# Splitting nearly every DMA transfer of a linear-attention and mixture-of-experts layer into smaller ones

## What is computed

```python
x = x + attn(layernorm(x), Wqkv, bqkv, Wout, bout, slopes)
x = x + ffn(layernorm(x), w_gate, wi_0, wi_1, wo)

# attn: q, k, v = split(x @ Wqkv + bqkv), per head, in blocks of the sequence
scores = einsum('bhid,bhjd->bhij', qb, kb) * intra_decay
o      = einsum('bhij,bhjd->bhid', scores, vb) + einsum('bhid,bhde->bhie', qb * q_decay, S)
S      = blk_decay * S + einsum('bhjd,bhje->bhde', kb * k_decay, vb)
# then out @ Wout + bout

# ffn: logits = x @ w_gate; the top 2 of 8 experts, weights = softmax(top 2 logits)
out = sum over the 2 experts of weight * ((silu(x @ wi_0[e]) * (x @ wi_1[e])) @ wo[e])
```

## Time and profile before

| | us |
|---|---|
| median of 3 runs | 6599.29 |
| lowest and highest run | 6589.15 and 6755.89 |
| the profiled execution | 6538.36 |
| its span on the slowest core (core 7) | 6536.4 |
| PE busy in the span | 3099.4 (47%) |
| DVE busy | 889.0 (14%) |
| ACT busy | 889.4 (14%) |
| DMA traffic | 732.70 MB, mean 112 GB/s |

### The profile page before, as it was taken

How to read it: one execution, slowest core, us unless ns; L and a number is a source line. 1 busy time by engine, 2 the same in 40 slices (tenths; PEclk the granted TensorE clock), 3 DMA queues, 4 the chain that set the end, 5 groups by cost and what they waited for, 6 DMA issues and landing times.

```text
span 6536.4 us, 39888 instructions; the slowest of 8 cores (6456.9 to 6536.4 us)
## 1 busy us (share of the span) xinstructions
PE 3099.4 (47%) x13620; PEld 1341.5 (21%) x13620; DVE 889.0 (14%) x1577; ACT 889.4 (14%) x2498; POOL 0.2 (0%) x4
## 2 busy tenths in 40 slices
PE   0002063063052142142637761444448888888887
PEld 0001021021021021021213320111113333333333
DVE  1111101101101101111010002221111111111111
ACT  1001012021021021030140011442110000000000
POOL 0000000000000000000000000000000000000000
PEclk9999575575575575565758885556769998999999
DMA  6664624514525425425211113002332111112111
GB/s 189 240 218 163 210 87 147 199 71 167 186 82 174 162 90 189 165 97 177 87 65 52 52 61 132 1 1 94 119 145 93 65 67 50 52 65 78 58 58 77
DMA packets 181569, 732.70 MB, mean 112 GB/s; under 512 B 13144, under 2 KB 13401, under 8 KB 142460
## 3 DMA queue, kind: packets, MB, share of 16 engines
q10 hardware_dynamic: 73728, 369.13, 16.4%
q1 hardware_dynamic: 107648, 361.03, 15.8%
HBM read 579.10 MB, written 151.01 MB: 112 GB/s over the span
## 4 chain that ended last, share of the span: by engine, by line
PE 42%; DMA 29%; ACT 10%; DVE 10%; issue 7%; ACTq 1%; SPq 0%; DVEq 0%
DMA s_cvf<-wffn_im 19%; PE pb L409 4%; PE pb L411 4%; PE pb L947 4%; DMA s_wqcf<-wqkv 4%; PE pb L949 4%; DVE s_cvb L298 4%; PE pb L903 3%; PE pb L904 3%; PE pb L905 3%; PE pb L906 3%; DMA s_wcg<-wqkvb 3%; PE pb L521 3%; PE pb L523 3%; PE pb L340 2%
## 5 line engine op out<-in xcount | busy, mean ns | idle before, releaser
L409 PE MATMUL pb<-s_wcg,s_lnT 128*128 128x512 bf16 x1536 | 610.4, 397 | 1315.8 <-ACT s_kvst L428 1143.2
L411 PE MATMUL pb<-s_wcg,s_lnT 128*128 128x512 bf16 x1536 | 608.5, 396 | 0.0
L340 PE MATMUL pb<-s_ident,s_lntile 128*128 128x128 bf16 x512 | 135.7, 265 | 984.6 <-ACT s_lntile L330 742.6
L947 PE MATMUL pb<-s_wo,s_inter 128*128 128x512 bf16 x1024 | 402.8, 393 | 237.8 <-DVE s_out L962 208.6
L409 PEld LDWEIGHTS pb<-s_wcg,s_lnT 128*128 128x128 bf16 x1536 | 156.2, 102 | 1521.8 <-issue 1357.1
L298 DVE CAST s_cvb<-s_cvf 128x2048 bf16<-128x2048 f32 x192 | 235.6, 1227 | 1419.0 <-DMA s_cvf<-wffn_im 1419.0
L903 PE MATMUL pb<-s_lnT,s_wi 128*128 128x512 bf16 x1024 | 394.7, 385 | 26.3 <-DMA s_wi<-wall 14.3
L949 PE MATMUL pb<-s_wo,s_inter 128*128 128x512 bf16 x1024 | 402.8, 393 | 0.0
L904 PE MATMUL pb<-s_lnT,s_wi 128*128 128x512 bf16 x1024 | 394.7, 385 | 0.0
L905 PE MATMUL pb<-s_lnT,s_wi 128*128 128x512 bf16 x1024 | 394.7, 385 | 0.0
L906 PE MATMUL pb<-s_lnT,s_wi 128*128 128x512 bf16 x1024 | 394.4, 385 | 0.0
(11 more groups left out here) (124 smaller groups left out, 2862.1 us busy)
## 6 DMA issues: line engine op xcount, KB each, us to landing
s_cvf<-wffn_im ACTq DMA_DIRECT2D x192, 1024.0 KB, 6.0
s_wcg<-wqkvb SPq DMA_DIRECT2D x60, 2048.0 KB, 12.3
wall<-s_cvb ACTq DMA_DIRECT2D x192, 512.0 KB, 2.9
s_wi<-wall ACTq DMA_DIRECT2D x128, 512.0 KB, 4.3
s_wqcf<-wqkv SPq DMA_DIRECT2D x16, 3072.0 KB, 15.4
s_wostr<-woutb SPq DMA_DIRECT2D x64, 512.0 KB, 3.4
s_wo<-wall SPq DMA_DIRECT2D x16, 2048.0 KB, 9.2
wqkvb<-s_wqcb SPq DMA_DIRECT2D x16, 1536.0 KB, 6.7
```

Of the source, the lines that this page charges most:

```text
L340: t.inc(ten.transpose(pbankb(bk, P), s_lntile[:, par * C + ch * P: par * C + (ch + 1) * P], s_ident[:]), pe)
L409: ten.matmul(pbank(2 * pt4, 512), lhs, s_wcg[:, i * KB:i * KB + 512], start=st_, stop=False)
L411: ten.matmul(pbank(2 * pt4 + 1, 512), lhs, s_wcg[:, i * KB + 512:(i + 1) * KB], start=st_, stop=False)
L947: ten.matmul(pbank(ybanks[0], 512), lhs, wosl[:, hc * KB: hc * KB + 512], start=st_, stop=sp)
```

## The change

Nearly every large transfer is issued as several smaller ones, each with its own completion increment on the same semaphore. Who issues, what is waited for, the buffers and the arithmetic stay. Transfers that move a row of a matrix per partition are cut by columns, so each piece still has 128 rows but shorter ones; the loads of `s_wcg` and `s_wo` are cut by blocks of rows, and their rows stay 2 KB.

| transfer | before | now | row before, now |
|---|---|---|---|
| load Wqkv | 3 MB | 6 x 0.5 MB | 24 KB, 4 KB |
| store wqkvb | 1.5 MB | 3 x 0.5 MB | 12 KB, 4 KB |
| load expert weights | 1 MB | 2 x 0.5 MB | 8 KB, 4 KB |
| store wall | 0.5 MB | 2 x 0.25 MB | 4 KB, 2 KB |
| load token tile (all three places) | 1 MB | 4 x 0.25 MB | 8 KB, 2 KB |
| load `s_wcg` half | 2 MB | 4 x 0.5 MB | 2 KB, 2 KB |
| load Wout, store woutb | 1 MB, 0.5 MB | 2 pieces each | halved |
| load `s_wostr` | 0.5 MB | 2 x 0.25 MB | 4 KB, 2 KB |
| store x1, load x1, store y | 1 MB | 2 x 0.5 MB | 8 KB, 4 KB |
| load `s_wi` (two per block) | 0.5 MB | 2 x 0.25 MB each | 4 KB, 2 KB |
| load `s_wo` | 2 MB | 4 x 0.5 MB | 2 KB, 2 KB |

The core of the diff (the other places are cut in the same way):

```diff
+    def dma2(eng, out_ap, in_ap, sem, cols, nsplit):
+        step = cols // nsplit
+        for k in range(nsplit):
+            t.inc(eng.dma_start(out=out_ap[:, k * step:(k + 1) * step],
+                                in_=in_ap[:, k * step:(k + 1) * step]), sem, 16)
+        return t.count[sem]
...
-        t.inc(sync.dma_start(out=s_wqcf[:, par * 3 * C:(par + 1) * 3 * C],
-                             in_=d_wqkv[i * P:(i + 1) * P, :]), dQp[par], 16)
+        dma2(sync, s_wqcf[:, par * 3 * C:(par + 1) * 3 * C],
+             d_wqkv[i * P:(i + 1) * P, :], dQp[par], 3 * C, 6)
...
-            t.inc(scal.dma_start(out=s_cvf[:, par * C:(par + 1) * C],
-                                 in_=d_wffn[i * P:(i + 1) * P, :]), dEp[par], 16)
+            dma2(scal, s_cvf[:, par * C:(par + 1) * C], d_wffn[i * P:(i + 1) * P, :],
+                 dEp[par], C, 2)
...
-            t.inc(scal.dma_start(out=d_wall[i * P:(i + 1) * P, :],
-                                 in_=s_cvb[:, par * C:(par + 1) * C]), dDp[par], 16)
+            for k in range(2):
+                t.inc(scal.dma_start(out=d_wall[i * P:(i + 1) * P, k * KB:(k + 1) * KB],
+                                     in_=s_cvb[:, par * C + k * KB: par * C + (k + 1) * KB]),
+                      dDp[par], 16)
...
-                src = d_wqkvb[hf * KB:(hf + 1) * KB, colbase:colbase + KB].rearrange(
-                    "(c p) n -> p c n", p=P)
-                dst = s_wcg[:, hf * 8 * KB:(hf + 1) * 8 * KB].rearrange("p (c n) -> p c n", n=KB)
-                t.inc(sync.dma_start(out=dst, in_=src), dWp[hf], 16)
+                for kk in range(4):
+                    src = d_wqkvb[hf * KB + kk * 2 * P: hf * KB + (kk + 1) * 2 * P,
+                                  colbase:colbase + KB].rearrange("(c p) n -> p c n", p=P)
+                    dst = s_wcg[:, (hf * 8 + 2 * kk) * KB:(hf * 8 + 2 * kk + 2) * KB].rearrange(
+                        "p (c n) -> p c n", n=KB)
+                    t.inc(sync.dma_start(out=dst, in_=src), dWp[hf], 16)
...
-        t.inc(scal.dma_start(out=s_wi[:, par * C:(par + 1) * C], in_=d_wall[r0:r0 + P, :]), dFp[par], 16)
+        dma2(scal, s_wi[:, par * C:(par + 1) * C], d_wall[r0:r0 + P, :], dFp[par], C, 2)
```

More of the change, by code:

```diff
@@ L274, in build_program @@
         t.wait(sync, dv, wq_cvt[i])
-        t.inc(sync.dma_start(out=d_wqkvb[i * P:(i + 1) * P, :],
-                             in_=s_wqcb[:, par * 3 * C:(par + 1) * 3 * C]), dQs[par], 16)
+        for k in range(3):
+            t.inc(sync.dma_start(out=d_wqkvb[i * P:(i + 1) * P, k * 2 * KB:(k + 1) * 2 * KB],
+                                 in_=s_wqcb[:, par * 3 * C + k * 2 * KB: par * 3 * C + (k + 1) * 2 * KB]),
+                  dQs[par], 16)
         wq_st[i] = t.count[dQs[par]]
@@ L367, in build_program @@
                 t.wait(sync, dv, ln_state["stats_dv"].get(pt - 2, 0))
-            t.inc(sync.dma_start(out=s_xstr[:, par * C:(par + 1) * C],
-                                 in_=d_xp[pt * P:(pt + 1) * P, :]), dXp[par], 16)
+            dma2(sync, s_xstr[:, par * C:(par + 1) * C], d_xp[pt * P:(pt + 1) * P, :],
+                 dXp[par], C, 4)
             x_ev[pt] = t.count[dXp[par]]
@@ L475, in build_program @@
             t.wait(sync, dv, own_stats[tt - 2])
-        t.inc(sync.dma_start(out=s_xstr[:, par * C:(par + 1) * C],
-                             in_=d_x[tt * P:(tt + 1) * P, :]), dXp[par], 16)
+        dma2(sync, s_xstr[:, par * C:(par + 1) * C], d_x[tt * P:(tt + 1) * P, :],
+             dXp[par], C, 4)
         xev = t.count[dXp[par]]
@@ L499, in build_program @@
             t.wait(sync, pe, wcg_user[0])
[L500 to L503, removed]
+            for kk in range(4):
+                src = d_wqkvb[hf * KB + kk * 2 * P: hf * KB + (kk + 1) * 2 * P,
+                              cg * KB:(cg + 1) * KB].rearrange("(c p) n -> p c n", p=P)
+                dst = s_wcg[:, (hf * 8 + 2 * kk) * KB:(hf * 8 + 2 * kk + 2) * KB].rearrange(
+                    "p (c n) -> p c n", n=KB)
+                t.inc(sync.dma_start(out=dst, in_=src), dWp[hf], 16)
             wcg_ld[hf] = t.count[dWp[hf]]
@@ L562, in build_program @@
             t.wait(sync, pe, qkv_mm_done[(5, 1)])
-        t.inc(sync.dma_start(out=s_cvf2[:, par * C:(par + 1) * C],
-                             in_=d_wout[i * P:(i + 1) * P, :]), dQp[par], 16)
+        dma2(sync, s_cvf2[:, par * C:(par + 1) * C], d_wout[i * P:(i + 1) * P, :],
+             dQp[par], C, 2)
         t.wait(vec, dQp[par], t.count[dQp[par]])
@@ L571, in build_program @@
         t.wait(sync, dv, wo_cvt[i])
-        t.inc(sync.dma_start(out=d_woutb[i * P:(i + 1) * P, :],
-                             in_=s_cvb2[:, par * C:(par + 1) * C]), dVw[par], 16)
+        for k in range(2):
+            t.inc(sync.dma_start(out=d_woutb[i * P:(i + 1) * P, k * KB:(k + 1) * KB],
+                                 in_=s_cvb2[:, par * C + k * KB: par * C + (k + 1) * KB]),
+                  dVw[par], 16)
         wo_st[i] = t.count[dVw[par]]
@@ L720, in build_program @@
                 t.wait(sync, pe, wostr_used[tpi * NCH + i - 2])
-            t.inc(sync.dma_start(out=s_wostr[:, wpar * C:(wpar + 1) * C],
-                                 in_=d_woutb[i * P:(i + 1) * P, :]), dGp[wpar], 16)
+            dma2(sync, s_wostr[:, wpar * C:(wpar + 1) * C], d_woutb[i * P:(i + 1) * P, :],
+                 dGp[wpar], C, 2)
             lev = t.count[dGp[wpar]]
@@ L764, in build_program @@
             t.wait(sync, dv, resid_ev[tt])
-            t.inc(sync.dma_start(out=d_x1[tt * P:(tt + 1) * P, :],
-                                 in_=s_x1t[:, par * C:(par + 1) * C]), dOp[par], 16)
+            for k in range(2):
+                t.inc(sync.dma_start(out=d_x1[tt * P:(tt + 1) * P, k * KB:(k + 1) * KB],
+                                     in_=s_x1t[:, par * C + k * KB: par * C + (k + 1) * KB]),
+                      dOp[par], 16)
             x1_dma[tt] = t.count[dOp[par]]
@@ L831, in build_program @@
             t.wait(sync, dDp[1], e_ffncv_st[1])
-        t.inc(sync.dma_start(out=s_out[:, tt * C:(tt + 1) * C], in_=d_x1[tt * P:(tt + 1) * P, :]), dS, 16)
+        dma2(sync, s_out[:, tt * C:(tt + 1) * C], d_x1[tt * P:(tt + 1) * P, :], dS, C, 2)
         seed_ev[tt] = t.count[dS]
@@ L854, in emit_wi_load @@
         r0 = e * 3 * M + hc * P
-        t.inc(scal.dma_start(out=s_wi[:, par * C:(par + 1) * C], in_=d_wall[r0:r0 + P, :]), dFp[par], 16)
+        dma2(scal, s_wi[:, par * C:(par + 1) * C], d_wall[r0:r0 + P, :], dFp[par], C, 2)
         r1 = e * 3 * M + M + hc * P
-        t.inc(scal.dma_start(out=s_wi[:, (2 + par) * C:(3 + par) * C], in_=d_wall[r1:r1 + P, :]), dFp[par], 16)
+        dma2(scal, s_wi[:, (2 + par) * C:(3 + par) * C], d_wall[r1:r1 + P, :], dFp[par], C, 2)
         wi_dma[(e, hc)] = (par, t.count[dFp[par]])
@@ L869, in emit_wo_load @@
         r0 = e * 3 * M + 2 * M
-        src = d_wall[r0:r0 + M, cs * KB:(cs + 1) * KB].rearrange("(h p) n -> p h n", p=P)
-        dst = s_wo[:, par * NHC * KB:(par + 1) * NHC * KB].rearrange("p (h n) -> p h n", n=KB)
-        t.inc(sync.dma_start(out=dst, in_=src), dGp[par], 16)
+        for k in range(4):
+            src = d_wall[r0 + k * 2 * P: r0 + (k + 1) * 2 * P,
+                         cs * KB:(cs + 1) * KB].rearrange("(h p) n -> p h n", p=P)
+            dst = s_wo[:, (par * NHC + 2 * k) * KB:(par * NHC + 2 * k + 2) * KB].rearrange(
+                "p (h n) -> p h n", n=KB)
+            t.inc(sync.dma_start(out=dst, in_=src), dGp[par], 16)
         wo_dma[(e, cs)] = (par, t.count[dGp[par]])
@@ L969, in build_program @@
         t.wait(sync, dv, y_evac[(NE - 1, tt, 1)])
-        t.inc(sync.dma_start(out=d_y[tt * P:(tt + 1) * P, :], in_=s_out[:, tt * C:(tt + 1) * C]),
-              dOp[tt % 2], 16)
+        for k in range(2):
+            t.inc(sync.dma_start(out=d_y[tt * P:(tt + 1) * P, k * KB:(k + 1) * KB],
+                                 in_=s_out[:, tt * C + k * KB: tt * C + (k + 1) * KB]),
+                  dOp[tt % 2], 16)
     if DEBUG_TAPS:
```

## The result

The split kernel is slower. Its runs against those of the kernel before, on the same chip, give a ratio of 1.030 with a 95% interval of 1.021 to 1.040; the medians of all runs are 6862.29 and 6666.71 us. On the 6599 us of the kernel before that the forecast used, 1.030 is some 6797 us. The forecast was 6640 us, range 6540 to 6745, and no change with a chance of 0.85.

What follows compares the result with a forecast made beforehand. The prediction took the 192-step expert conversion loop to bound the kernel, then PE after 4877 us. Its terms summed to +41 us, 6579 for the profiled execution; carried to the median 6599 that gave 6640, range 6540 to 6745.

Steps and rivals of the forecast that it cites:

- Row length: Expert conversion loop: shorter rows move bytes slightly slower, +0.05 us a step, +10 us over 192 steps.
- The signs that I named: Forecast wrong if conversion step grows 0.4 us or more, or a second piece lands more than its bytes behind the first.
- the pairs: Two `s_wi` or `s_wcg` loads issued closely: the second costs only its bytes, so queued transfers stream without a gap.
- Issue: Expert conversion loop: the extra store and load issues are covered by bytes already queued, 0 us a step.
- Rival 1: Transfers start only as fast as issued: 0.82 us a conversion step, +291 us in all, 6890; chance 0.07.
- rival 2: Each added transfer pays a fixed 2.2 us that does not overlap: +845 us over 192 steps, 7440; chance 0.03.
- Wqkv, +5: Wqkv conversion, 16 steps: slower byte rate of shorter rows, +0.3 us a step, +5 us.
- Rival 4: Long rows were the brake: Wqkv -51 us, conversion loop -19, in all -44, 6555; chance 0.08.
- Wout and scan, +2: Wout conversion: same pattern as the expert loop, 16 steps at 0.1 us, +2 us.
- Experts, output projection, `s_wcg`: Later activation at experts' ends +6 us, shorter `s_wostr` rows +4, extra completion writes of `s_wcg` loads +2.
- the ends of the bursts: Conversion loop is left 12 times, ACT's next instruction behind the extra store issue, 0.41 us each: +5 us.
- Beside each other: Conversion loop meeting `s_wcg` loads: its shorter rows get a smaller share of the DMA engines, +7 us of at most +71.

Runs made afterwards that it cites:

- ahead: Kernel before, unsplit, with the expert conversion issuing load i+1 ahead of the wait for cast i: 6111.76 us against 6503.24.
- contig_halves: Kernel before with the expert conversion's load and store each in two pieces, each a contiguous DRAM range: step 7.66 us, undisturbed times 6465.35 and 6479.64 against 6469.54.
- conv_both: Kernel before with only the expert conversion's load and store split into column halves: step 8.61 us, median 6742.32 us against 6615.38.
- all_but_conv: Split kernel without the expert conversion's two splits: step 7.68 us, six times from 6514.56 to 6857.01 us, total not settled.

## Why the prediction was wrong

- **What bounds the kernel: right.** The conversion loop with its 192 steps, latency after latency. The run "ahead" shows it from the other side.
- **The step that failed is "Row length", +0.05 us a conversion step.** I bounded it by the byte rates of rows of 2, 4 and 8 KB in full flow and by the quickest pair of 0.5 MB loads. Two readings were weak. The window for 4 KB rows, 398.90 to 399.60, holds packets of a store to `wall`, not of a load. And the 425 GB/s of 8 KB rows are of a stretch of the Wout load; in the conversion loop the load's first 2 us have 290, and its bytes flow over 3.9 us and not 2.47. All of those rows were of transfers that covered their addresses without a gap, or with the pitch of 12 KB of `wqkvb`, an odd number of 4 KB chunks. A column half has the same row length but starts every row at the same remainder by 8 KB. The term measured +0.8 a step in the median (7.8 to 8.6), half of it by the load and half by the store; the stage became 125 us longer in place of 10. The signs that I named agree: the step grew by more than 0.4 and the idle time of the cast, 1518.6, left its 1400 to 1450, while the sign on the second piece did not come, since it lands its bytes behind the first. So the pairs were read rightly and the transfers do stream; what was missing is a slower start of the reads by their addresses.
- **Issue, 0 a step: right.** The two extra issues are there (load 2.2 in place of 1.7 after the cast), and contig_halves has them too at 7.66. Rival 1 gave 0.82 a step, very near what was measured, but for another reason; by the time alone it would have been taken for proven. Its other terms did not come: `s_wcg` +5.9 and not +42.
- **The fixed part of a transfer, rival 2: refuted**, and with it the reading of the rule of the Trainium skill ("Rules for kernel authors" in DMA: Bandwidth & Descriptors, at least 1 MiB in a DMA) as a price per transfer. Two pieces of half a MB in place of one cost nothing in contig_halves.
- **Wqkv, +5: too small, +20 measured.** The cause stays open. Its pieces take 4 KB of every 24 KB, an even number of 4 KB chunks, so it may be the same; but the first load piece is also issued 5.1 us after the cast's start in place of 3.9, behind three store issues in place of one, and 16 x 1.2 would be 20 by itself. Neither was tried. Rival 4 (long rows were the brake) had the wrong sign.
- **Wout and scan, +2: +11 measured**, with the same column halves in load and store; 16 steps at 0.8 would be 13.
- **Experts, output projection, `s_wcg`:** +6, +4, +2 forecast, +6.9, +3.1, +5.9 by the rows above. The sizes are near, which shows no more than that: no run isolates them, what a completion write costs was not measured, and the +5 for the ends of the bursts was not tested either.
- **Beside each other, +7:** conv_both has the same stage as the full change (2887 and 2886), and all_but_conv has 26 us less than before. Splitting the `s_wcg` loads took nothing from the conversion; why the stage is shorter was not followed up.

What the memory does with such addresses no trace here shows. A page of the Trainium skill (DMA: Bandwidth & Descriptors, "Latency and other measured facts") reports slow copies at row pitches of 2 MiB and more and infers that rows fall on the same channels; here it shows at pitches of 8 and 16 KB with rows of 4 KB, and not at 12 KB. Whether the 4 KB grain is one of channels or banks stays open, and so does why only the start of a load is slow.

## What to carry to other kernels

When a transfer is cut, ask first whether anything was waiting for a part of it. Nothing was here, since every wait stayed on the last piece. If it must be cut, cut it into pieces that are contiguous in DRAM and not by columns: the same number, size and packet length cost 0.8 us of 7.8 in one case and nothing in the other. A loop of load, compute, store that stands in one queue gains from issuing the next load ahead of the wait, and that took 8% off this kernel.

## What had not been expected of the hardware

- A load of 4 KB rows starts slowly when all its rows start at the same remainder by 8 KB: 8.20 against 7.8 us a step, and with the store split too 197 GB/s against 290 in the first 2 us. Later in the same load the rate reaches 389. With a stride of three chunks of 4 KB nothing is lost.
- Writes of 2 KB out of every 4 KB are through no later (3.7 us after the cast's start, 3.8 before), and slow the reads that follow them: 8.26 us a step.
- A load to 64 of the 128 partitions runs at 220 GB/s with all DMA engines busy, half the 425 of one to 128.
- An issue can take long by itself when several pieces are issued behind one another: the median issue of the six Wqkv pieces takes 1102 ns, against 383 for the one transfer before. In the split kernel:

```profile
L201 SPq DMA_DIRECT2D s_wqcf<-wqkv x96: 354/1102/2226, 25.2 to 351.8; - x96
```
